# One attention and feed-forward kernel: value rows sent through the output projection ahead of the softmax, router and half chunk turned round

## The reference, cut to what matters

```python
# first layer, on z = layernorm(x)
q = z @ wq.T;  k = concat(ctx, z @ wk.T);  v = concat(ctx, z @ wv.T)
attn = softmax(q @ k.T * scale)
x = x + tanh(g0) * ((attn @ v) @ wo.T)
# second layer
x = x + tanh(g) * ((silu(z @ w1q.T) * (z @ w3q.T)) @ w2q.T)   # weights are ternary, 682 hidden columns
# third layer: running maxima, exponents, a scan over 64 rows, a quotient
# fourth layer
probs = softmax(z @ router_w);  top 2 of 8 -> combine
x = x + tanh(g) * (shared(z) + sum_e combine[:, e] * expert_e(z))
```

## Time and profile before

| what | value |
|---|---|
| median of 3 runs | 811.12 us (810.39 to 813.89) |
| profiled execution, span from the first to the last instruction | 806.8 us |
| the runs' median less that span | 4.3 us |
| PE busy | 741.4 us, 92% |
| DVE busy | 633.1 us, 78% |
| POOL busy | 398.0 us, 49% |
| ACT busy | 384.9 us, 48% |

### The profile page before, as it was taken

One profiled execution on the slowest core, in us unless ns is written; L12 is line 12 of the kernel. 1 busy time (PEld: TensorE's weight loads), 2 busy tenths in 40 slices (PEclk: granted clock), 3 DMA queues, 4 the chain that ended last, 5 costly groups with the idle time before them and its releaser, 6 DMA issues.

```text
span 806.8 us, 13118 instructions
## 1 busy us (share of the span) xinstructions
PE 741.4 (92%) x4582; PEld 642.7 (80%) x4582; DVE 633.1 (78%) x1043; ACT 384.9 (48%) x730; POOL 398.0 (49%) x382
## 2 busy tenths in 40 slices
PE   6988799889999999989998999989998999968896
PEld 5876687778888788878887888878887988746785
DVE  2857589687978798888989798888979797899532
ACT  3536434556355644654455645653465635431321
POOL 1024332364746365464636465455546464565364
PEclk8999979999999999999999999999999999988999
DMA  8170002010022013110032113110121000101121
GB/s 249 53 208 1 1 1 53 27 54 27 27 79 67 27 38 81 45 47 13 26 78 66 35 30 78 55 37 26 43 74 53 26 26 26 41 26 40 34 73 51
DMA packets 35895, 41.19 MB, mean 51 GB/s; under 512 B 3118, under 2 KB 27096, under 8 KB 35864
## 3 DMA queue, kind: packets, MB, share of 16 engines
q1 hardware_dynamic: 35864, 40.78, 17.6%
HBM read 36.45 MB, written 4.33 MB: 51 GB/s over the span
## 4 chain that ended last, share of the span: by engine, by line
PE 59%; DVE 15%; issue 4%; POOL 3%; ACT 1%; DMA 1%; DVEq 0%; POOLq 0%; ACTq 0%
PE sums L475 14%; PE gate_ps L475 13%; PE up_ps L475 12%; PE transit L475 6%; DVE wk L1389 3%; DVE wk L1394 3%; PE transit L540 3%; PE transit L467 3%; PE transit L552 3%; DVE wk L1396 2%; POOL act_sb L1139 2%; PE transit L520 1%; POOL hid_l L1130 1%; DVE act_sb L1379 1%; DVE za_l L1333 1%
## 5 line engine op out<-in xcount | busy, mean ns | idle before, releaser
L1130 POOL TENSOR_TENSOR hid_l<-act_sb,hid_h 128x512 fp32r<-128x512 f32 (+1 forms) x128 | 173.3, 1354 | 171.9 <-ACT hid_h L917 171.9
L917 ACT ACTIVATE hid_h<-act_sb 128x512 fp32r<-128x512 f32 (+1 forms) x128 | 80.4, 628 | 150.9 <-POOL act_sb L1139 117.8
L1139 POOL TENSOR_TENSOR act_sb<-act_sb,late 128x512 f32<-128x512 f32 x64 | 92.0, 1438 | 100.2 <-DVE act_sb L1381 80.9
L1379 DVE SCALAR_TENSOR_TENSOR act_sb<-act_sb,gate_ps 128x512 f32<-128x512 f32 (+1 forms) x128 | 85.8, 670 | 68.9 <-ACT act_sb L901 68.9
L475 PE MATMUL sums<-down_h,hid_h 128*128 128x256 f32 x320 | 92.3, 288 | 12.7 <-POOL hid_l L1130 12.7
L475 PE MATMUL sums<-down_h,hid_l 128*128 128x256 f32 x320 | 90.0, 281 | 0.0
L475 PE MATMUL sums<-down_l,hid_h 128*128 128x256 f32 x320 | 90.0, 281 | 0.0
L1381 DVE TENSOR_TENSOR act_sb<-act_sb,up_ps 128x512 f32<-128x512 f32 x120 | 82.4, 687 | 4.1
L901 ACT ACTIVATE act_sb<-gate_ps 128x512 f32<-128x512 f32 x80 | 47.2, 590 | 71.4 <-PE up_ps L475 66.1
L475 PEld LDWEIGHTS sums<-down_h,hid_h 128*128 128x128 f32 x320 | 60.9, 190 | 19.8 <-issue 17.9
L475 PE MATMUL gate_ps<-zm_h,gate_h 128*128 128x512 f32 x140 | 62.3, 445 | 5.6 <-DVE act_sb L1381 5.6
(11 more groups left out here) (194 smaller groups left out, 1962.7 us busy)
## 6 DMA issues: line engine op xcount, KB each, us to landing
late<-combine_rows SPq DMA_DIRECT2D x64, 256.0 KB, 3.2
ctx_tok<-in_ctx SPq DMA_DIRECT2D x8, 512.0 KB, 4.9
vals<-in_ctx SPq DMA_DIRECT2D x16, 256.0 KB, 5.6
out_x<-late SPq DMA_DIRECT2D x8, 512.0 KB, 3.2
xa<-in_x SPq DMA_DIRECT2D x7, 512.0 KB, 3.5
wk<-in_L_ffn_w SPq DMA_DIRECT2D x2, 682.0 KB
late<-in_L_ffn_w_down SPq DMA_DIRECT2D x1, 1024.0 KB, 6.6
wk<-in_L_ffn_w_gate SPq DMA_DIRECT2D x2, 512.0 KB, 4.4
```

Source lines behind the costliest of these rows:

```text
L917: nc.scalar.activation(hid_h[0:n, pos], act_sb[0:n, pos], ACT.Copy).then_inc(hid_h_set, 1)
L1130: nc.gpsimd.tensor_tensor(hid_l[0:n, pos], act_sb[0:n, pos], hid_h[0:n, pos].bitcast(F32), ALU.subtract).then_inc(hid_l_set, 1)
L1139: nc.gpsimd.tensor_tensor(act_sb[:, pos], act_sb[:, pos], comb_sb[:, pos], ALU.mult).then_inc(weighted, 1)
L1379: nc.vector.scalar_tensor_tensor(mine, mine, 1.0, gate_ps[pos][0:hidden_rows(chunk)], ALU.add, ALU.mult).then_inc(gated_one, 1)
```

## The change

The output projection goes onto the value rows instead of onto the attended rows. Once, in turn 0, the product of the value weights and `wo` is made on PE (`turn_wv`, `fuse_wv_wo`) and takes the place of the value weights. In each block the context rows are multiplied by `wo` on PE (`context_out`, 16 products of 256 columns, each into one half of the partitions), and ACT copies them to where SP loaded them before; the two loads go. `attend` then gives the projected rows at once (8 products of 256 columns, again in halves); `project` and ACT's two copies between the two go. `context_out` stands behind `values` on PE and on ACT.

The router's product has the weights (padded to 32 columns) as the stationary side and the high and low parts of z as the moving one, four row tiles into four quarters of the partitions; ACT copies the result (`keep_logits`), PE turns it (`logits_T`, in the place of `keep_clock(3)`), and DVE's `route` loses its first two instructions. The turning of the combine weights is one instruction instead of four.

The half chunk A5 keeps its low part in the upper 64 partitions, with the weight rows there twice, so that its `down` has four products instead of eight; the low part is made by DVE (`low_tail`) instead of by POOL.

DVE makes the low parts of z between the two halves of `exponents`; they stood behind both halves and the gate of chunk M3.

```diff
 TRANSIT = [
...
-    ("A", "q0"), ("A", "q1"), ("A", "k0"), ("A", "k1"), ("A", "v0"), ("A", "v1"), ("A", "scores"), ("A", "pT"),
-    ("A", "oT0"), ("A", "oT1"), ("A", "wo0"), ("A", "wo1"), ("A", "z1T0"), ("A", "z1T1"), ("W", "yT0"), ("W", "yT1"),
-    ("W", "z3T0"), ("W", "z3T1"), ("W", "route"),
+    ("A", "q0"), ("A", "q1"), ("A", "k0"), ("A", "k1"), ("A", "v0"), ("A", "v1"), ("A", "u0"), ("A", "u1"),
+    ("A", "scores"), ("A", "pT"), ("A", "wo0"), ("A", "wo1"), ("A", "z1T0"), ("A", "z1T1"), ("W", "yT0"), ("W", "yT1"),
+    ("W", "z3T0"), ("W", "z3T1"), ("W", "route"), ("W", "logits"),
...
-                    sp.dma_start(vals[S:P, :, 0], ctx_seqs[t.i, 0]).then_inc(ctx_val_in, 16)
-                    sp.dma_start(vals[0:S, :, 1], ctx_seqs[t.i, 1]).then_inc(ctx_val_in, 16)
...
+            def fuse_wv_wo():
+                pe.wait_ge(fuse_kept, 1)
+                pe.wait_ge(wo_in, 16)
+                for k in range(KH):
+                    for m in range(KH):
+                        last = nc.tensor.matmul(up_ps[0][:, k * D:(k + 1) * D], wv_turned[:, m, k * P:(k + 1) * P], wo[:, m],
+                                                start=m == 0, stop=m == KH - 1)
+                last.then_inc(fuse_done, 1)
+
+            def context_out(t):
+
+                wait_taken(pe, t, "A", "ctxT0", "ctxT1", claims=("A", "u0"))
+                for pair in range(2):
+                    bank, full = claim(t, "A", f"u{pair}")
+                    for r in range(2):
+                        for k in range(KH):
+                            for q in range(2):
+                                last = nc.tensor.matmul(bank[(1 - q) * S:(2 - q) * S, r * D:(r + 1) * D], keys[:, k, 2 * pair + r, 1 + q],
+                                                        wo[:, k], start=k == 0, stop=k == KH - 1)
+                    last.then_inc(full, 1)
...
             def attend(t):
...
+                            last = nc.tensor.matmul(bank[q * S:(q + 1) * S, r * D:(r + 1) * D], probsT[:, cols], vals[:, tile, q],
+                                                    start=True, stop=True)
                     last.then_inc(full, 1)
...
             def route(t):
...
+                for k in range(KH):
+                    for a, z in enumerate((z_h, z_l)):
+                        for r in range(NT):
+                            last = nc.tensor.matmul(bank[r * RW:(r + 1) * RW, 0:P], route_w[:, k], z[:, k, r * P:(r + 1) * P].bitcast(F32),
+                                                    start=k == 0 and a == 0, stop=k == KH - 1 and a == 1, tile_position=(0, r * RW))
                 last.then_inc(full, 1)
...
                 q_and_k(t)
                 values(t)
+                context_out(t)
                 m_down(3)
                 scores(t)
...
                 attend(t)
                 m_up(6)
-                if first:
-                    keep_clock(3)
-                project(t)
                 m_up(7)
...
                 down(t, ("A", HC - 2))
-                keep_clock(3)
+                if w:
+                    logits_T(t)
+                else:
+                    keep_clock(3)
                 down(t, ("A", HC - 1))
...
+            def context_out(t):
+                for pair in range(2):
+                    bank = wait_full(act, t, "A", f"u{pair}")
+                    for q in range(2):
+                        half = slice((1 - q) * S, (2 - q) * S)
+                        last = nc.scalar.activation(vals[half, 2 * pair:2 * pair + 2, q],
+                                                    bank[half].rearrange("p (r d) -> p r d", r=2), ACT.Copy)
+                    last.then_inc(free_of("A", f"u{pair}"), 1)
...
                 squash(t, ("A", HC - 1))
+                if w:
+                    keep_logits(t)
                 high_hidden(t, ("A", HC - 1))
...
+            def low_tail(t):
+
+                pos = CHUNKS.index(("A", HC - 1)) % 2
+                n = chunk_no(t, ("A", HC - 1))
+                dve.wait_ge(hid_h_set, n)
+                dve.wait_ge(hid_l_set, n - 1)
+                nc.vector.tensor_tensor(hid_h[HALF:P, pos], act_sb[0:HALF, pos], hid_h[0:HALF, pos].bitcast(F32), ALU.subtract).then_inc(hid_l_set, 1)
...
-                    for h in range(KH):
-                        exponents(t, h)
+                    exponents(t, 0)
+                low_parts(t, "A", "z0T", za_h, za_l, za_h_set, 0, 2 * KH)
+                if w:
+                    exponents(t, 1)
                 m_gate(3)
-                low_parts(t, "A", "z0T", za_h, za_l, za_h_set, 0, 2 * KH)
...
                 gate(t, ("A", HC - 1))
+                low_tail(t)
```

More of the change, by code:

```diff
@@ L532, in attend @@
             def attend(t):
-                wait_taken(pe, t, "A", "v0", "v1", "pT", claims=("A", "oT0"))
-                pe.wait_ge(ctx_val_in, t.count("A", 32, 32))
-                for h in range(KH):
-                    bank, full = claim(t, "A", f"oT{h}")
-                    for r in range(NT):
-                        for q in range(2):
-                            cols = slice((2 * r + q) * S, (2 * r + q + 1) * S)
-                            last = nc.tensor.matmul(bank[:, cols], vals[:, r, q, h * P:(h + 1) * P], probsT[:, cols],
-                                                    start=True, stop=True)
-                    last.then_inc(full, 1)
[L544 to L547, removed]
+                wait_taken(pe, t, "A", "v0", "v1", "u0", "u1", "pT", claims=("A", "wo0"))
                 for pair in range(2):
@@ L609, in combine_T @@
                 bank, full = claim(t, "M", "combT")
-                for r in range(NT):
-                    last = nc.tensor.transpose(bank[0:E, r * P:(r + 1) * P], combine[:, r], ident[:])
-                last.then_inc(full, 1)
+                nc.tensor.transpose(bank[0:NT * E, 0:P], combine[:].rearrange("p e r -> p (e r)"), ident[:]).then_inc(full, 1)
             def down(t, chunk):
@@ L937, in turn @@
                 if first:
-                    for name in ("wq", "wk", "wv"):
-                        high(name)
+                    high("wq")
+                    high("wk")
+                    keep_wv()
                 m_chunk(0)
@@ L950, in turn @@
                 normalise(t, "A", 1, xa, za_row, rstd_a, shift_a)
+                if first:
+                    high("wv")
                 m_chunk(3)
@@ L973, in turn @@
                     readouts(t, 1)
-                attend(t)
                 if first:
-                    high("route")
                     high("down")
@@ L1025, in second @@
                     decays(t, h)
-                readouts(t, 0)
-                attend(t)
-                readouts(t, 1)
+                for h in range(KH):
+                    readouts(t, h)
                 normalise(t, "A", 2, rows, za_row, rstd_a, shift_a)
@@ L1182, in turn @@
                 m_low(9)
-                for c in range(HC):
+                for c in range(HC - 1):
                     if w and c == 2:
@@ L1450, in route @@
             def route(t):
-                bank = wait_full(dve, t, "W", "route")
-                both = bank[:, 0:2 * NT * E].rearrange("p (r a e) -> p r a e", r=NT, a=2)
+                bank = wait_full(dve, t, "W", "logits")
+                scores = bank[:, 0:P].rearrange("p (r a) -> p r a", r=NT)[:, :, 0:E]
                 step = [0]
```

114 lines of the change are left out of this document (64 added, 50 removed).

## The result

The changed kernel takes 852.78 us (median of 4 runs, 852.52 to 855.38) against 812.5 for the kernel before: 1.0503 times as long, interval 1.0472 to 1.0535. The profiled execution spans 850.8 us, 44.0 more than the 806.8 of before; the medians lie 40.3 apart. The forecast was 846.

What follows compares the result with a forecast made beforehand. PE's work and DVE's chain, both 20.0 us from the `up` of M5 to the turned z, were taken to bound it together. Span 806.8 + 30 + 3.2 + 0.3 + 1 = 841.3, plus 4.3: 846 us; range 820 to 871.

Steps and rivals of the forecast that it cites:

- End of the turn: Router and half chunk: PE through 1.1 us sooner, DVE 0.45 us later by `low_tail`; the 1.1 us become a wait.
- Low parts: Low parts of z: the 2.0 us wait moves from ahead of the queries to ahead of the keys, less 0.2.
- Context rows: Ahead of the `up` of M5: 1.2 us wait, then `context_out` 3.45 us; that `up` ends 4.45 us later.
- The chain: From the `up` of M5 to the turned z: 20.0 us, keeps every instruction; PE's 5.0 us saved become waits.
- Its collision: POOL's low part of M5 falls on DVE's additions at L1426: up to 1.1 us more on the chain.
- From there to the end of the turn PE's work is dense as before.: Behind the turned z, itself 4.45 to 5.55 us later, PE's work stays dense; 5.0 us a turn, 30 for six.
- the 93 to 95 that were to show the mechanism: Sign in the changed profile: a turn of the loop should last 93 to 95 us.
- Outside the loop: Turn 0: +4 less 0.8 for the half chunk; turn 1: 0.3; the router's turn in turn 8: +1 us.
- halves one by one: Rival: products into halves of the partitions run one by one, 3.1 us more per block; about 870 us; chance 0.08.
- No waits behind ACT: Rival: ACT reaches queries and value rows in time, 2.0 us a turn; 828 us; chance 0.18.
- PE's count: Rival, faster: chain behind M5 shorter than 20.0 us, turn shrinks 5.5 us with PE's work; 783 us; chance 0.09.

Runs made afterwards that it cites:

- 811.87: Kernel before with the change's router and half chunk alone: attention part undone, low parts of z back behind both halves of the exponents; 811.87 us, 1.0019 of before.
- 804.42: Kernel after with its attention part undone; router, half chunk and new place of the low parts stay; 804.42 us, 0.9891 of before.
- the run at 840.97: Kernel after with ACT's high part of M5 behind the squash of M6 instead of ahead of it; 840.97 us, 1.0359 of before.
- 844.72: Kernel after with eight products nobody reads on PE, in its wait ahead of the turned z; 844.72 us, 1.0409 of before.
- 840.04: Kernel after with ACT's copies of the queries ahead of the high part of M3 and the squash of M4; 840.04 us, 1.0343 of before.
- the best kernel with all of the change: Kernel after with `context_out` behind the `up` of M6 and ACT's high part of M5 behind the copies of the context rows; 806.36 us, 0.9916 of before.

## Why the prediction was right, step by step

*End of the turn.* Right in its effect. PE's saving became a wait of 0.94 us ahead of the `up` of M2. DVE's extra 0.45 us did not come: from the half chunk's gate (ending at 437.11) to `add_sums` it is 5.29 us, before 5.34, since the subtraction ahead of the exponential (L1512, then L1465) took 0.19 us instead of 0.74.

```profile
436.42 0.69 DVE L1422 TENSOR_TENSOR act_sb<-act_sb,gate_ps 64x512 f32<-64x512 f32 x1
438.00 0.69 DVE L1430 TENSOR_TENSOR hid_h<-act_sb,hid_h 64x512 fp32r<-64x512 f32 x1 [0.89 <-ACT hid_h L950]
...
442.40 1.41 DVE L1409 SCALAR_TENSOR_TENSOR x<-sums,gain_f,xa 128x512 f32<-128x512 f32 x2
```

*Low parts.* Right in kind: the wait moved from ahead of the queries to ahead of the keys. It is 1.25 instead of 1.8, and the keys start 0.76 us sooner instead of 0.2; the 0.45 us that did not come would explain most of this, which no run shows by itself. The pair 811.87 and 804.42 shows what the new place is worth.

*Context rows.* Right: a wait of 0.98 (1.2 forecast), 3.67 us (3.45), the squash of M5 4.28 later (4.45). The two moves behind the `up` of M5 and of M6 show that this is the heart of the loss.

*The chain.* Right that it keeps its length and PE's savings turn into waits: 1.82 ahead of the `up` of M8, 2.35 ahead of z; a third, 1.28 for POOL's low part between the two, was not forecast. Its collision was sized at half of "up to 1.1" and came whole, 1.12; the run at 840.97 shows it, with this addition at its own length. DVE's addition and POOL's low part of M5:

```profile
393.86 1.79 DVE L1475 TENSOR_TENSOR wk<-wk 128x512 f32<-128x512 f32 x1
```

```profile
393.35 1.76 POOL L1169 TENSOR_TENSOR hid_l<-act_sb,hid_h 128x512 fp32r<-128x512 f32 x1
```

The addition starts 0.51 us behind POOL's instruction and ends 0.54 behind it. The Trainium skill (SBUF — State Buffer, "two separate sides") has the one that comes first hold the shared port pair to its end; the trace agrees, since what is left of the addition behind POOL, 0.54 us, is near its own 0.68.

*"From there to the end of the turn PE's work is dense as before."* This is the step that failed: 37.82 instead of 36.41 us. The new waits cost a second time, through the clock that PE gets when it goes on, a term that the sum doesn't have; 844.72, with the clock held at 1.00 and 36.25 us, shows it. With it a turn is 6.8 us longer in turns 3 to 6, not 5.0, and six turns 38.1 us, not 30; the turn of 95.68 us also lies above the 93 to 95 that were to show the mechanism.

*Outside the loop.* 2.6 for turns 0 and 1 (3.5 forecast). Turn 8 costs 2.7 instead of 1 (72.2 us, before 69.45). In seven of the twelve kernels with the new router it takes 70.45 to 70.9 us, in the other five, this one among them, 72.2 to 72.4. In all five the clock falls in the turn's first 6 us (a mean of 0.73 here), but in three of the seven it does so too; where the last 1.4 us come from stays open. The last turn costs about 0.6 more, in all twelve.

The median is 7.2 us above the sum of 845.6: 8.1 in the six turns and 2.3 in turns 8 and 9, less 0.9 in turns 0 and 1, and less 2.3 because the median lies only 2.0 above the span, not 4.3. This last part is luck: by span alone the forecast was 9.5 us short. Of the rivals, halves one by one (870) is refuted by the 3.67 us. No waits behind ACT (828) is refuted by the waits of 1.25 and 0.98 us, and 840.04 shows that without most of them the time is still far above 828. PE's count (783) is refuted by the 9.87 us for which PE is idle in the turn; even in the best kernel with all of the change it is busy for only 83.29 of the 88.05 us of a turn.

## What to carry to other kernels

Before taking work from a busy engine, follow the chain that starts at its last product and ends at its next wait: where that chain is as long as the engine's own work, a product put ahead of it costs its full length, and the same product inside it costs nothing (852.8 and 806.4 us for the same instructions in two orders; about 6.7 of the difference are the collision). Each new wait on PE needs a look at the clock that follows it, and each instruction that comes sooner on ACT a look at which instruction of DVE POOL will then run beside.

## What the runs showed of the hardware

Products into two halves of the partitions run side by side though their weights take all 128 rows: 32 of 256 columns take 3.67 us, 0.115 each, where a full one takes 0.204; `attend` has 0.122. By the Trainium skill (TensorE: Matmul & The Clock Gate, "Part 3") weight loads overlap a running product only where the row group differs; read as in the prediction, the halves would then have run one by one, and the measurement decides against that. By the Trainium skill (TensorEngine Tiling (Array Packing), "Key Properties") tiles load and multiply in parallel; the trace agrees, with 0.115 against 0.204 us.

In the kernel after the clock falls behind the turned z in turns 3 to 6, with waits of 1.82, 1.28 and 2.35 us ahead of it in the turn shown. In turns 2 and 7 it falls earlier and not behind z. PE's waits in that stretch of turn 2, and its clock behind the `up` of M8 and behind z:

```profile
211.25 0.57 PE L479 MATMUL gate_ps<-zm_h,gate_h 128*128 128x512 f32 x1 [1.83 <-DVE act_sb L1422]
219.52 1.09 PE L471 MATMUL transit<-ident,zqo 128*128 128x128 f32 x8 [2.25 <-ACT zqo L824]
```

```profile
212.00:215.00 3.00, 3.00 (x8) 2.32 (x7) 2.77 (x8) 1.12 (x2) 3.00 (x3) 0.51 0.15 58
219.90:223.90 4.00, 4.00 (x25) 3.48 (x24) 3.64 (x6) 2.11 (x6) 2.59 (x2) 1.00 0.20 68
```

The half clock (0.51) lies here where PE has time to spare: the wait of 1.28 us is gone, z comes 21.00 us behind the squash as in the other turns, and nothing is lost. With `context_out` behind the `up` of M5, where the wait of 2.0 us ahead of z stands alone, the clock falls in one turn of the six (90.78 us, the others 89.0 to 89.3). What tells the turns in which it falls behind z from those in which it doesn't stays open.
